# Attention products of two steps written in alternation on TensorE, and no filling matmuls in its waits

## What is computed

```python
scores = jnp.einsum('bqhd,bkhd->bhqk', q, k) / jnp.sqrt(jnp.float32(D)).astype(h.dtype)
top_s, top_i = jax.lax.top_k(scores, TOPK)
attn = jax.nn.softmax(top_s, axis=-1)
...
o = jnp.einsum('bhqk,bhqkd->bqhd', attn, vg).reshape(B, L, C)
return o @ w_co + b_co
```

## Time and profile before

| | before |
|---|---|
| median of 3 runs | 670.6 us (669.71 to 672.51) |
| the profiled execution's own time | 665.29 us |
| its span, first to last instruction | 663.5 us |
| TensorE's mean granted clock | 0.863 of full |
| PE busy / DVE busy / ACT busy / POOL busy | 570.0 / 490.9 / 386.3 / 306.4 us |
| products of L1536 and L1566, together | 204.5 us of PE busy time |
| filling products L1473 | 150, 27.4 us of PE busy time |

### The profile page before, as it was taken

The page is one execution under the profiler, slowest core; times in us unless marked ns, Lnnn a source line. Parts: engine busy times, 40 slices in busy tenths (PEclk is TensorE's granted clock), DMA queues, the critical chain, the costliest instruction groups (busy, mean ns, idle before and its releaser), DMA issues.

```text
span 663.5 us, 14489 instructions
## 1 busy us (share of the span) xinstructions
PE 570.0 (86%) x5152; PEld 378.9 (57%) x5152; DVE 490.9 (74%) x1291; ACT 386.3 (58%) x669; POOL 306.4 (46%) x584
## 2 busy tenths in 40 slices
PE   3888989899999999999998889786999987867477
PEld 3645556566756565657665556554655664634246
DVE  2577767853859687745377727999999999999953
ACT  2546878799696887886757766452233531611133
POOL 6884535435845444364562446641341446111133
PEclk9858999999999999998989979777575795765779
DMA  9560344302333533020335043140020002000000
GB/s 319 143 159 3 88 106 112 73 2 54 76 67 69 105 77 78 2 65 2 66 72 123 2 129 68 28 101 0 2 65 2 2 10 64 9 1 2 1 2 16
DMA packets 15062, 39.23 MB, mean 59 GB/s; under 512 B 2641, under 2 KB 6801, under 8 KB 14737
## 3 DMA queue, kind: packets, MB, share of 16 engines
q0 software_dynamic: 8960, 29.37, 20.1%
q1 hardware_dynamic: 5312, 8.46, 3.8%
q10 hardware_dynamic: 720, 0.49, 0.3%
HBM read 7.96 MB, written 0.52 MB: 13 GB/s over the span
## 4 chain that ended last, share of the span: by engine, by line
DVE 38%; PE 37%; ACT 8%; DMA 6%; issue 6%; POOL 4%; ACTq 0%; POOLq 0%
PE psum L1590 10%; DVE left L1419 8%; DVE left L1429 7%; DVE top L1426 6%; DVE top L1416 6%; DVE maxima L1406 5%; PE psum L1566 5%; PE psum L1536 5%; ACT softmax_T L1298 4%; DMA qk_stack<-centred 3%; PE psum L1625 3%; PE psum L1636 3%; DMA qk_stack<-qk_parts 2%; DVE maxima L1402 2%; PE psum L1617 2%
## 5 line engine op out<-in xcount | busy, mean ns | idle before, releaser
L1298 ACT ACTIVATE softmax_T<-psum 128x1024 f32<-128x1024 f32 (+1 forms) x224 | 210.9, 962 | 111.7 <-PE psum L1577 73.3
L1406 DVE TENSOR_REDUCE maxima<-psum 128x4 f32<-128x1024 f32 x160 | 190.1, 1216 | 52.4 <-PE psum L1536 51.6
L1566 PE MATMUL psum<-qk_stack 32*128 32x256 f32 (+1 forms) x896 | 114.9, 346 | 28.1 <-DMA qk_stack<-centred 9.6
L1590 PE MATMUL psum<-softmax_T,values 128*32 128x256 f32 (+1 forms) x1792 | 129.9, 408 | 4.8 <-ACT softmax_T L1298 3.5
L1566 PEld LDWEIGHTS psum<-qk_stack 32*128 32x128 f32 x896 | 72.3, 202 | 71.0 <-issue 31.0
L1227 POOL TENSOR_SCALAR unpicked<-left 128x512 bf16<-128x512 f32 x64 | 39.5, 616 | 136.0 <-DVE left L1429 135.3
L1536 PE MATMUL psum<-qk_stack 32*128 32x256 f32 (+1 forms) x768 | 89.6, 335 | 9.2 <-ACT softmax_T L1298 2.4
L1536 PEld LDWEIGHTS psum<-qk_stack 32*128 32x128 f32 x768 | 58.9, 200 | 37.5 <-issue 16.5
L1590 PEld LDWEIGHTS psum<-softmax_T,values 128*32 128x32 f32 x1792 | 56.7, 118 | 40.3 <-issue 12.0
L1187 POOL TENSOR_TENSOR qk_parts<-qk_parts 128x256 fp32r<-128x256 f32 x56 | 40.9, 730 | 77.0 <-ACT qk_parts L1281 76.6
L1158 POOL DMA_DIRECT2D qk_stack<-qk_parts x112 | 63.7, 580 | 7.0 <-POOL qk_parts L1187 6.3
(11 more groups left out here) (99 smaller groups left out, 870.3 us busy)
## 6 DMA issues: line engine op xcount, KB each, us to landing
qk_stack<-qk_parts POOLq DMA_DIRECT2D x112, 256.0 KB, 5.1
weights<-in_w SPq DMA_DIRECT2D x1, 1408.0 KB, 13.5
row_biases<-in_rows SPq DMA_DIRECT2D x1, 1088.0 KB, 10.8
weights<-in_w SPq DMA_DIRECT2D x2, 512.0 KB, 5.9
weights<-in_w SPq DMA_DIRECT2D x1, 832.0 KB, 9.0
qk_stack<-centred SPq DMA_DIRECT2D x48, 8.0 KB
weights<-in_w SPq DMA_DIRECT2D x1, 768.0 KB, 4.3
weights<-in_w SPq DMA_DIRECT2D x1, 576.0 KB, 3.7
```

Of the source, the lines that this page charges most:

```text
L1298: nc.scalar.activation(pT[:, slot, u % 2, :, 0:cols].rearrange("p (i t) n -> p i t n", t=NT), two_banks(step).rearrange("p i (t n) -> p i ...
L1406: nc.vector.tensor_reduce(rows[:, u // 4, u // 2 % 2, g:g + 2, :], ps.rearrange("p i (t k) -> p i t k", t=NT), AX_X, ALU.max).then_inc(fin, 1)
L1566: ins = nc.tensor.matmul(ps[:, i, t, 0:P if window else N], QKS[b][32 * g:32 * g + 32, s, 1, P * t:P * t + P], QKS[b][32 * g:32 * g + 32, ...
L1590: ins = nc.tensor.matmul(misc[32 * g:32 * g + 32, queries], V[:, b, t, first:first + 32], pT[:, slot, g // 2, 2 * (g % 2) + t, 0:P if wind ...
```

## The change

The weaving: when the planner has picked a scores, topk or weights step (weights not of layer 6, scores not of layer 5) and another such step of disjoint row groups is ready within 0.15 us (`TOGETHER`), it takes both. Their halves stand in alternation: tile 0 of the first, tile 0 of the second, tile 1 of the first, tile 1 of the second. TensorE waits for the banks and inputs of both ahead of the first product. The planner gives such a pair 0.5 us (`WOVEN`), less 0.1 where it stands beside the step ahead of it. The full products of scores, weights and topk are now all issued by one helper, `half` (L1498 for topk, L1505 for the others). In the program of after, 81 pairs are woven: 22 scores with scores, 34 scores with weights, 16 weights with weights of full layers, 6 weights with weights of layer 5, 3 topk with weights of layer 5. 78 of the pairs stand ahead of the first topk product.

The filling products: the loop that issued them is gone. The planner still counts them as there (`spare`), in its clock too.

The dependencies of scores and weights steps in the planner are those that the two alternating steps need, `("pool", "stack")` is planned at 0.62 us instead of 1.0, and the tables `LEAD`, `BIAS` and `EXTRA` have new numbers, so that every engine's list has another order.

```diff
-    ("act", "context", 0, 1): -13.2, ("act", "context", 0, 2): 4.2, ("act", "context", 0, 6): -9.8,
...
+WOVEN, WOVEN_BESIDE, WOVEN_FIRST, WOVEN_SECOND, WOVEN_SLOWER, TOGETHER = 0.5, 0.1, 0.46, 0.52, 1.5, 0.15
...
+        if eng == "pe" and weaves(step):
+            others = [(rank(n), c[0], n) for n in ready["pe"] if (c := choose(n)) is not None]
+            fit = [o for o in others if weaves(o[2][1]) and not groups(o[2]) & groups(t) and o[1] <= s + TOGETHER]
...
+        if other is not None:
+            s = max(s, at)
+            d = WOVEN - (WOVEN_BESIDE if beside(t, s) else 0.0)
...
-                for _ in range(SPARE.get(step, 0)):
-                    nc.tensor.matmul(psum[:, SLOT["bank", step][0], 0:2 * P], ident[:].bitcast(BF16)[:, 0:P],
-                                     ident[:].bitcast(BF16), start=True, stop=True)
-                if kind == "mods":
+                if weaves(step):
+                    inputs_in(step)
+                    if step in WOVEN_WITH:
+                        other = WOVEN_WITH[step]
+                        banks_free(pe, other)
+                        inputs_in(other)
+                        half(step, 0)
+                        half(other, 0)
+                        half(step, 1).then_inc(fin, 1)
+                        half(other, 1).then_inc(done[other[0], "pe"], 1)
+                    else:
+                        half(step, 0)
+                        half(step, 1).then_inc(fin, 1)
```

More of the change, by code:

```diff
@@ L558 @@
+    ("pool", "topk", 3, 3): -0.8, ("pool", "topk", 3, 5): -0.1, ("pool", "topk", 3, 6): 46.4,
+    ("pool", "topk", 3, 8): 48.1, ("pool", "z", 0, 0): 1.7, ("pool", "z", 0, 2): 2.6, ("pool", "z", 0, 3): -14.4,
[28 rows of a table added]
 }
 BIAS = {
-    ("act", "context"): -21.7, ("act", "heads_out"): 106.1, ("act", "k_parts"): 0.8, ("act", "maxima"): 50.3,
-    ("act", "mix"): 11.5, ("act", "normed"): -5.7, ("act", "qk"): -12.8, ("act", "up"): -16.3,
-    ("act", "values"): -25.6, ("act", "weights"): -7.5, ("dve", "divide"): -11.8, ("dve", "down"): 86.8,
@@ L574, in w_group, with weaves @@
+    ("pe", "weights"): 0.1, ("pool", "gated"): -0.6, ("pool", "k_parts"): 24.7, ("pool", "pre"): -0.9,
+    ("pool", "qk"): -7.4, ("pool", "stack"): 0.3, ("pool", "topk"): 106.6, ("pool", "z"): -3.5,
+    ("sp", "load"): -10.1, ("sp", "maxima"): -22.8, ("sp", "store"): 296.7,
+}
+def weaves(step):
+    kind, b, l, u = step
+    if kind == "topk":
+        return True
+    return kind == "scores" and ATTN[l]["kind"] == "full" or kind == "weights" and ATTN[l]["kind"] != "topk"
 def w_group(blk):
@@ L843, in choose, with hold, landing @@
         return s, taken
+    def hold(t, taken):
+        for ring, which in taken:
+            slots[ring] = [o for o in slots[ring] if o not in which]
+            slot[ring, t[1]] = [k for _, k, _ in which]
+            had[ring, t[1]] = sorted({before for _, _, before in which if before is not None})
+    def landing(t, land, end):
+        for r, taker in gives(t):
+            slots[r] += [(land + HOP, k, taker) for k in slot[r, taker]]
+            slots[r].sort()
+        for n in users[t]:
+            waiting[n] -= 1
+            ready_at[n] = max(ready_at[n], land + (HOP if n[0] != t[0] or land > end else 0.02))
+            if not waiting[n]:
+                ready[n[0]].append(n)
     left = len(order)
@@ L891, in plan @@
         lists[eng].append(step)
-        for ring, which in taken:
-            slots[ring] = [o for o in slots[ring] if o not in which]
-            slot[ring, step] = [k for _, k, _ in which]
-            had[ring, step] = sorted({before for _, _, before in which if before is not None})
         land = end + lag
```

527 lines of the change are left out of this document (268 added, 259 removed), and 330 rows, old and new, of tables (EXTRA, LEAD).

## The result

The changed kernel took 693.96 us (median of 4 runs, 686.53 to 698.6), the kernel before beside it 671.56 us (4 runs, 669.71 to 673.53): a ratio of 1.030, with a 95% interval of 1.020 to 1.040. The medians are 22.4 us apart, and the ratio stands for 19.9 us: every ratio here leaves out runs more than 1.5% above the fastest of their kernel (slow runs), here the one of 698.6 us, while the medians are of all runs. 671.0 us was forecast and 682 was the upper end.

The account below looks back on a forecast made before the run. TensorE bounds about 66 to 408 us, DVE the topk stage, then a mixed tail. First head 415.6 + topk stage 219.8 = 635.4; + tail 26.7 + 1.5 + 0.3 = 663.9 us span, median 671.0 us, range 661 to 682.

Parts of the forecast that it names:

- The alternation priced at 0: Paired steps on TensorE: the chip already interleaves ready steps by itself, so weaving their products was counted as 0 us.
- The second rival: Woven pairs save about 0.22 us each on TensorE; half of 17 us comes through, median 658 to 666; chance 0.24.
- Woven, both would wait ... The end stays: Pair at 79.46 us: joined start at 79.59, next step still at about 80.03, first step's result 0.13 us later.
- the third rival: Joint waits hold up first steps: 78 pairs by 0.30 us, a third on the chain, 8 us, median 679; chance 0.22.
- 8.0 us moved ahead of the first head, less 3.4 for more pairs: TensorE before DVE's first topk head: moved work adds 8.0 us, eight more pairs save 3.4; start 411.0 becomes 415.6 us.
- The topk stage, 225.8 to 219.8: First to last topk head, where DVE is the bound: 6.0 us of DVE's work moves ahead, shortening the stage.
- the case that the last sentence of the prediction named: The sum is wrong in its base if DVE waits for topk products between heads at a low clock.
- TensorE would just keep up: Topk stage without filling products: at half clock throughout, TensorE's remaining work would take at most 221 us of 229.
- The filling products, +1.5: Their removal costs nothing in the topk stage, and 1.5 us through the clock in the tail, between ends 0 and 10.6.
- the dense work is five sixths of it and lifts the clock alone: Tail: the mix and divide, 1.96 + 1.11 us against 0.61 of filling products, would raise TensorE's clock without the latter.
- The tail's order, +0.3: Tail: one batch's down step now stands ahead of the last batch's up steps, counted as 0.3 us longer.
- The clock ahead of the first head, priced at nothing: From about 66 to 408 us TensorE ran at clock 0.98; the sum had no term for a lower clock there.

Follow-up runs that it names:

- a_fill: The changed kernel with the 164 filling products its planner would place, pairs still woven: 687.45 us, ratio 1.025 to the kernel before.
- a_plain_fill: The changed kernel with its new lists, no pair woven, and the filling products where its planner has them: 680.78 us, 10.5 over the kernel before.
- a_plain: The changed kernel with its new lists, no pair woven and no filling products: 683.41 us, ratio 1.016 to the kernel before.
- b_woven: The kernel before, lists and filling products kept, with 117 neighbouring pairs woven (joint wait, alternating halves): 684.24 us, ratio 1.021.
- b_joint: The kernel before with the same 117 pairs waiting jointly, but products in the old order, four of one step then four of the other: 684.42 us.
- b_ready: The kernel before with only the 38 pairs woven that already ran interleaved in its trace: 672.27 us, against 670.27 for the kernel before beside it.
- b_nofill: The kernel before without its 150 filling products and nothing else changed: 676.61 us, ratio 1.004.
- b_early: The kernel before with 15 more filling products in TensorE's waits from 27.5 to 41.1 us: 671.63 us, ratio 1.000.

## Why the prediction was wrong, point by point

The medians add up along one path: before 671.54, less filling products 676.61 (+5.1), plus new lists 683.41 (+6.8), plus weaving 693.96 (+10.6, measured apart from this set). That is 22.4 us. By the ratios the same three are 2.6, 8.2 and 9.1, 19.9 us. By the other path, lists with filling products +10.5, then weaving +6.7 (a_fill against a_plain_fill, from two sets), then no filling products +6.5. Each part is known to some 3 to 6 us, and the filling products' alone isn't resolved on the lists of before. The weaving is the surest: 10.6 and 12.7 us by a_plain and b_woven, 6.7 by a_fill. The lists, +6.8 to +10.5, are not much smaller.

**The alternation priced at 0: right.** b_joint and b_woven differ by 0.2 us in the median, and by 0.02 us over the 75.6 us of the same work. The chip interleaves ready steps by itself, as the earlier trace rows shows, and a woven ready pair lets the next step in after 0.44 us (195.18 to 195.62), as forecast. The second rival fell with it.

The Trainium skill, page "TensorE: Matmul & The Clock Gate", Part 3, "The mechanism", says that products start and end strictly in program order. If they did, 117 pairs would have gained 0.22 us each on b_joint's order, some 26 us of TensorE; the two kernels took the same, so the trace disagrees here too.

**"Woven, both would wait ... The end stays": this step failed.** I followed one pair in which the second step was 0.13 us late and let the joined pair start at 79.59, 0.06 us behind ACT's end, as the second step had done alone. Such a pair starts 0.24 us behind the signal, not 0.04, so the next step does move: over the 87 woven pairs that ran between 56 and 366 us of the kernel before, a pair with its wait, up to the next step's start, takes 0.77 us on average apart, 0.89 in b_woven and 0.87 in b_joint (these two with somewhat more half clock in it). I also gave the later first result no price, though it moves further, by the lateness as well (0.67 us in the pair above), and DVE and ACT, which free banks for later steps, wait for it. How much each of the two costs is not separated. What isn't lost is the time in which TensorE stands: joined, both steps need only 0.44 us once they start. At full clock the whole comes to 5.8 us in 69.8 (8%), and where only ready pairs are joined to 0.2 us (b_ready).

The trace of before had the sizes: only 33 of 99 pairs ran interleaved, and 35 were late by more than 0.25 us. I had put the later results in as the third rival, with 78 pairs by 0.30 us, a third of it on the path, 8 us and a chance of 0.22. It measured 10.6 to 12.7: the mechanism in its main line, without the slower start, and nearly the size. Its signs came true as well, a first head behind 420 us and DVE and ACT less busy ahead of it (62 and 73% of 377 us, against 66 and 78%), though the lists and the clock had a part in these. It should have been the likeliest case, because two thirds of the pairs had a late partner by my own count.

**8.0 us moved ahead of the first head, less 3.4 for more pairs: not confirmed.** In the profiles a_plain's first head starts 6.4 us behind b_nofill's (423.4 and 417.0), near the +4.6 that was forecast, but a_plain_fill's starts 14.6 behind that of before (425.6 and 411.0), though in that comparison too only the lists differ. From 66 us to the head TensorE waits no more in a_plain than before (22.6 and 22.5 us idle); it is busy 334.8 us in place of 322.5, with 48.7 us at half clock in place of 17.1. So moved work and a lower clock stand in the 12.4 us together, and these runs don't part them. The 20 us from 423.4 up to 443.3 came with the weaving, and with the clock of that execution.

**The topk stage, 225.8 to 219.8: mis-sized.** It took 222.9 us, and 225.6 in a_plain. The busy times of DVE over the stage, columns as before. The changed kernel:

```profile
443.30:666.20 222.90, 151.89 (x1078) 98.41 (x1082) 213.88 (x815) 69.19 (x114) 69.48 (x121) 0.61 0.07 17
```

a_plain:

```profile
423.40:649.00 225.60, 156.79 (x1077) 100.83 (x1080) 214.08 (x815) 69.39 (x114) 69.46 (x121) 0.58 0.07 17
```

the kernel before:

```profile
411.00:636.80 225.80, 177.80 (x1318) 117.48 (x1320) 218.98 (x822) 77.06 (x131) 75.46 (x133) 0.70 0.10 23
```

DVE lost 5.1 us of work, close to the 6.0 I had counted. But its idle time rose from 6.8 us to 9.0, and to 11.5 in a_plain. a_plain's waits of DVE in the stage:

```profile
DVE top L1434 <- PE psum L1498: 2.3, 4, 1.3
DVE x L1466 <- PE psum L1659: 1.3, 1, 1.3
DVE softmax_T L1474 <- PE psum L1667: 1.2, 2, 0.9
DVE rden L1453 <- PE psum L1641: 0.8, 1, 0.8
```

In the kernel before only the last of these waits is there, also 0.8 us, besides the first head's; the changed kernel has 3.2 us in six such waits. So TensorE, at a clock of 0.58 to 0.61, no longer quite keeps up, the case that the last sentence of the prediction named. "TensorE would just keep up" was worked out over the whole stage, and the waits are those of single steps in it.

**The filling products, +1.5: too low in the tail.** The tail is 3.0 us longer without them on the lists of before (29.7 and 26.7 us), 4.9 in the woven and 2.4 in the unwoven kernel of the new lists (30.6 and 25.7, 30.5 and 28.1). Over the whole kernel their absence measured 5.1 us by the medians and 2.6 by the ratio on the lists of before (not resolved), 6.5 and 3.4 on the new ones (2.6 on a_plain's, unresolved), inside the ends of 0 and 10.6. The argument that the dense work is five sixths of it and lifts the clock alone was wrong in the tail: the mix at 665.16 and the divide at 667.74 run at half clock, as in the earlier trace rows, but TensorE then idles 0.62 us for ACT, and the next mix is slow again (1.80 us) where the kernel before ran at full clock from 639.28 us on the earlier trace rows. The Trainium skill, same page, Part 1, "What's actually happening", has the half clock as the default that activity lifts; the tail agrees (12.5 us of half clock without filling products, 0 in a_fill), while in b_early products put into a few waits did not keep it up.

**The tail's order, +0.3:** a_plain's tail is 30.5 us, b_nofill's 29.7, so +0.8; the difference is small.

**The clock ahead of the first head, priced at nothing.** The changed kernel was at half clock for 78.7 us there, before 17.1, b_woven 42.2. Each run's time at half clock follows from its span and mean clock (2 x span x (1 - clock)). Across the runs of one and the same kernel a straight line gives a span that rises by 0.23 us (before, 13 runs), 0.28 (b_woven) and 0.29 us (a_plain and the changed kernel) per us at half clock. By that the changed kernel's 61.6 us more would be some 14 to 18 of the 32 us by which its first head is late in this profile. That is a correlation, over a whole program of which DVE covers the longest stretch at half clock, and with four runs each the lines are loose (0.18 in a_fill, 0.46 in b_joint). Where TensorE is the bound a us costs more. The same 20 instructions of DVE, first in the kernel before, then in b_nofill, where the clock was at half for 13.1 us of it:

```profile
125.92:140.86 14.94, 13.64 (x146) 9.26 (x144) 11.16 (x21) 13.09 (x20) 5.16 (x11) 1.00 0.01 3
127.79:148.31 20.52, 19.46 (x148) 11.88 (x146) 11.27 (x22) 13.24 (x20) 5.15 (x11) 0.68 0.01 2
```

That is 5.6 us for 13.1 at half clock, 0.43 each. I cut the way from DVE's 21st instruction to the first head at every 20th and compared piece by piece. Pieces in which both kernels are at full clock throughout take 219.5 us before and 228.1 in b_woven, nearly 9 us by the waits alone; the other pieces take 182.7 and 192.3, with 24.3 us more at half clock. From a_plain to the changed kernel the first kind goes from 192.4 to 198.2 us, +5.8, the other from 221.9 to 236.7, +14.9, with 29.9 us more at half clock. So the waits cost without the clock in both, while in the changed kernel nearly three quarters of the 20.7 us lie where the clock was low too. Whether the waits brought the clock down is not shown: b_nofill, with no more waits, had 20.1 us more at half clock than before. How much of the changed kernel's loss goes by way of the clock stays open.

## What to carry to other kernels

A wait for two inputs in front of joined work holds back the earlier one's result by the lateness of the later, and here the joined work also started 0.2 us later behind the signal than a lone step. Count how many pairs are ready together in the trace (here a third), and expect a loss if most are not and the engine is the bound. To compare two kernels with the same lists, cut the stretch at the same instructions, not at the same times. Before interleaving instructions by hand, look whether the trace has them interleaved already: start times that cross program order say so. Filling products belong into the thin places of TensorE that are on the path, here the tail, where they were worth 2.4 to 4.9 us.

## What the runs showed of the hardware that I had not expected

- Eight products of two steps on different row groups take 0.51 us in the order A0 A1 B0 B1 and in A0 B0 A1 B1, and 117 such pairs make no difference in the kernel's time (684.42 and 684.24 us; 75.58 and 75.56 us over the same work at full clock).
- A joined pair that was held by DVE or ACT starts 0.23 to 0.25 us behind the signal in 30 of 40 cases of b_woven, a lone second step 0.04 behind it in 39 of 41 of before.
- In a stretch where TensorE is the bound, 13.1 us at half clock made the same work 5.6 us longer (20.52 against 14.94 us).
- The time at half clock differs between executions of one kernel, and the span follows it by 0.23 us per us in the kernel before, though DVE covers most of it. At nearly one mean amount (203 and 210 us) two kernels differed by 12.7 us, so the half clock summed over the program ranks no kernels.
- Fifteen filling products in TensorE's waits of 27 to 41 us did not keep the clock up: 20.5 us at half in place of 27.3 (b_nofill, without them, has 20.5 too), and 671.63 us against 671.36.
